# Two transposes of the mixed rows moved ahead of two weight chunks, and one pair of copies moved ahead of another

## The chip, the cores and the metric

The kernel runs on one core of one Trainium2 chip. The metric is the device time of one execution, in microseconds. The core has five engines that run their own instruction lists and meet through semaphores: TensorE (PE in the profile, its weight loads PEld), VectorE (DVE), ScalarE (ACT), GpSimd (POOL) and SyncE (SP), which here only issues DMAs.

## The reference, cut to what matters

```python
x = L0_attn_x                                  # (2, 1024, 128): two sequences
xn = _layernorm(x)
s = _L0_attn_ref(xn, ...)                      # gated recurrence with a scan over time
g = _silu(_L0_ffn_ref(xn, ...))                # six layers of local attention and FFN
return x + s * g

# inside _L0_ffn_ref, for each of the 6 layers
x = attn_layer(shift_tokens(x), Wqkv[i], q_scale[i], k_scale[i], Wo[i]) + x
x = ffn_layer(shift_tokens(x), ln_g[i], ln_b[i], W1[i], b1[i], W2[i], b2[i]) + x

def shift_tokens(t):        # the second half of the columns comes from the token before
    a, s = jnp.split(t, 2, -1)
    s = jnp.pad(s, ((0, 0), (1, 0), (0, 0)))[:, :-1]
    return jnp.concatenate([a, s], -1)
# attn_layer: qkv = x @ Wqkv (128 -> 3 * 1024), 16 heads of 64, l2norm and rotary on q and k,
# softmax within windows of 32 tokens and the window before, times v, @ Wo
```

Everything is computed in float32; the products for q, k, v and the first FFN product are made of three products of split operands (high and low parts).

## The kernel before, in words

The two sequences are two streams, b = 0 and 1. Each is cut into 8 tiles of 128 tokens. A step i is one tile of one layer, so there are 48 steps, and each step has two halves, one for each stream. Every engine has a function half(i, b) that writes out its work of that half by hand, in order; the engine executes it in that order. The stages of the pipeline lie side by side: in half (i, b) TensorE makes q, k, v of tile i (qkv, six chunks of 512 columns: 0 and 1 are q, 2 and 3 are k, 4 and 5 are v), transposes k and q of tile i - 1 (transpose_keys, transpose_qk) and makes its scores, transposes the probabilities of tile i - 2 (transpose_probs), multiplies them with v (probs_v) and projects (out_projection), and does the FFN of tile i - 4 (ffn_up, down_chunks). From step 40 on the recurrence of the other branch is worked in (the rec_ functions).

The "mixed rows" are the tile of x with the shifted half of its columns. SP copies the shifted half in with three DMAs (shift_x, x<-x in the profile) in the half before. transpose_mixed(i, b) transposes them for the next half: stream 1 of the same step in the half of stream 0, stream 0 of the next step in the half of stream 1 (next_tile). ScalarE's evac_mixed copies the transpose out twice, as xsh and rounded as xs_hi; GpSimd's low_x makes the low part xs_lo, and with that chunk 0 of the next half may start.

PSUM banks are handed out in pairs by written orders. tr_order is that of the two banks ps_tr: in each half probs 0, probs 1, qk 2, qk 3, mixed, qk 0, qk 1, and "rows" in stream 1. The n-th fill takes bank n % 2, and TensorE waits in ring_free until the fill before it in the same bank has been copied out (tr_done). pv_order does the same for ps_pv and qn_order for ps_qn (chunks 0 to 5, with the recurrent ones between 3 and 4). Neither order is changed.

Of the other functions named below: evac_k copies the transposed keys out of ps_tr (kT, L1184), evac_pv the result of P times V (oT, L1175), evac_q the transposed queries (qT, L1195), square writes the squares of a chunk (sq, L1166), exps is ScalarE's exponential of the scores (L1201). VectorE's rotate reads a chunk twice (t and qk, L1535 and L1538) once square has been done, and so frees its bank. ffn_gate (hid, L1661) is its product in the FFN, which frees the bank of ffn_up. On GpSimd the two additions of a half (qk, L2016), the scalings (qkr, L2028) and floor (floored, L1986) matter here.

Of the kernel before, what the change touches and what calls it, by code (L numbers as in the profile page):

```python
# [91 lines left out]
def valid(step):  # L92

    return not step.fixed or 0 <= step.n < STEPS
# [269 lines left out]
def layers(nc, a, x, xmid, branch, ident, eps_col, w, rec):  # L364

    with ExitStack() as ctx:
# [145 lines left out]
        def first_half(i, b):  # L512
            return i.first and b == 0
# [37 lines left out]
        with nc.Block() as block:  # L551
# [191 lines left out]
            def _(pe):  # L743
# [30 lines left out]
                def qkv(i, b, chunks):  # L774
                    if not valid(i):
                        return
                    if 0 in chunks:
                        pe.wait_ge(xs_ready[b], i.n + 1)
                    if not first_half(i, b):
                        pe.wait_ge(lo_ready[chunks[0] // 2], (i.layer + 1) * w.splits(chunks[0] // 2))  # L780
                    for c in chunks:
                        if first_half(i, b) and c == 1:
                            transpose_input([1], ps_pv[1])
                        if first_half(i, b):

                            part = c // 2
                            pe.wait_ge(*((lo_ready[part], w.splits(part)) if c % 2 else (lo_ready[part], 1) if part == 2 else (first_low, part + 1)))
                        bank = next_bank(i, ("qkv", b, c))
                        place = w.split_place(i.layer, c // 2, c % 2)
                        part = slice(place, place + COLS)  # L790
                        mm(ps_qn[bank][:, :], xs_hi[b][:, :], w_hi[:, part], start=True, stop=False)  # L791
                        mm(ps_qn[bank][:, :], xs_hi[b][:, :], w_lo[:, part], start=False, stop=False)  # L792
                        mm(ps_qn[bank][:, :], xs_lo[b][:, :], w_hi[:, part], start=False, stop=True).then_inc(qn_full[bank], 1)  # L793
# [67 lines left out]
                def probs_v(i, b, f):  # L861
                    j = i - 2
                    if not valid(j):
                        return
                    if j.first:
                        pe.wait_ge(s_xT, 6)
                        pe.wait_ge(cleared, 1)
                    if f == 0:
                        pe.wait_ge(v_moved[b], (j.n + 1) * V_MOVE)
                        pe.wait_ge(v_carried[b], (j.n + 1) * V_CARRY)  # L870
                    wait_fill(pe, tr_done, tr_order, i, ("probs", b, f))
                    bank, n = fill(pv_order, i, ("pv", b, f))
                    ring_free(pe, pv_done, bank, n)
                    for g in (2 * f, 2 * f + 1):
                        for w in range(WINDOWS):
                            for hp in (2 * g, 2 * g + 1):
                                last = mm(pv_target(bank, hp, w), v_win[b][:, w, hp * DH:(hp + 1) * DH],  # L877
                                          pbd[:, hp, :, WINDOW * w:WINDOW * (w + 1)], start=True, stop=True)
                    last.then_inc(pv_full[bank], 1)
# [127 lines left out]
                def half(i, b):  # L1007
                    transpose_probs(i, b, 0)
                    transpose_probs(i, b, 1)
                    qkv(i, b, (0, 1))  # L1010
                    if (i.n, b) == (1, 1):
                        transpose_pair(1)
                    out_projection(i, 1 - b)
                    transpose_keys(i, b)
                    if b == 0:
                        probs_v(i, b, 0)
                        probs_v(i, b, 1)
                    qkv(i, b, (2, 3))
                    if b == 1:
                        probs_v(i, b, 0)  # L1020
                        probs_v(i, b, 1)
                    if i.first and b == 0:
                        pe.wait_ge(s_xT, 1)
                        transpose_input(range(B, HEAD), ps_pv[0])
                    transpose_mixed(i, b)
                    mask(i, b)
                    rec_hidden(i, b)
                    rec_gate_projection(i, b)
                    if (i.n, b) == (1, 1):
                        transpose_pair(2)  # L1030
                    transpose_qk(i, b, 0)
                    rec_output(i, b)
                    rec_rates(i, b)
                    transpose_qk(i, b, 1)
                    if b == 0:
                        ffn_up(i, 0)
                        ffn_up(i, 1)
                    qkv(i, b, (4, 5))
                    if (i.n, b) == (1, 0):
                        transpose_pair(0)  # L1040
                    if b == 0:
                        ffn_up(i, 2)
                    else:
                        transpose_rows(i)
                    scores(i, b, 0)
                    scores(i, b, 1)
# [63 lines left out]
            def _(act):  # L1110
# [257 lines left out]
                def half(i, b):  # L1368
                    new_layer = i.t == TILES - 1 and b == 1 and not i.last_layer
                    root_first = b == 0 and (i.t > 0 or i.first)  # L1370
                    if root_first:
                        inverse_root(*norm_tile(i, b), i - 3)
                    evac_probs(i, b, 0)
                    if not root_first and not i.first:
                        inverse_root(*norm_tile(i, b), i - 3)
                    square(i, b, 0)
                    evac_probs(i, b, 1)
                    square(i, b, 1)
                    if not root_first and i.first:
                        inverse_root(*norm_tile(i, b), i - 3)  # L1380
                    if i.first and b == 0:
                        split_first(4)
                        split_first(5)
                    if (i.n, b) in ((1, 0), (1, 1)):
                        normalise_pair(2 * b)
                    exps(*softmax_tile(i, b))
                    if new_layer:
                        split_high(i.layer + 1, 0)
                    evac_k(i, b, 0)
                    evac_k(i, b, 1)  # L1390
                    if b == 1:
                        square(i, b, 2)
                        square(i, b, 3)
                        normalise_rows(i)
                    evac_pv(i, b, 0)
                    evac_pv(i, b, 1)
                    if b == 0:
                        square(i, b, 2)
                    evac_mixed(i, b)
                    if b == 0:  # L1400
                        square(i, b, 3)
                    if b == 0 and valid(i - 4):
                        nc.scalar.preload_act_table(ACT.Gelu)
                    rec_gelu(i, b)
                    rec_decay(i, b)
                    rec_output(i, b)
                    evac_q(i, b, 0)
                    rec_tanh(i, b)
                    if b == 0:
                        ffn_gelu(i, 0)  # L1410
                    evac_q(i, b, 1)
                    if b == 0:
                        ffn_gelu(i, 1)
                    evac_v(i, b, 4)
                    if b == 0:
                        ffn_gelu(i, 2)
                    if (i.n, b) == (0, 1):
                        input_guess(1)
                    if (i.n, b) == (3, 0):
                        softplus_exp()  # L1420
                    evac_v(i, b, 5)
                    if b == 0 and valid(i - 4):
                        nc.scalar.preload_act_table_set("natural_log_exp_and_others")
                    if b == 1:
                        evac_rows(i)
                    rec_beta_log(i, b)
                    rec_beta_half(i, b)
                    if new_layer:
                        split_high(i.layer + 1, 1)
                    if b == 1:  # L1430
                        if i.t == 3:
                            round_w1(i.layer)
                        if i.t in (5, 6) and not i.last_layer:
                            split_high(i.layer + 1, 2, i.t - 5)
                    if (i.n, b) == (1, 0):
                        normalise_pair(1)
# [840 lines left out]
```

## Time and profile before

| | |
|---|---|
| median of 3 runs | 1550.27 us (1549.19 to 1552.37) |
| the profiled execution | 1548.62 us |
| its span, first to last instruction | 1546.8 us |
| TensorE busy | 1499.9 us, 97% |
| ScalarE, GpSimd, VectorE busy | 1346.7, 1291.4, 1283.4 us |
| mean granted clock of TensorE | 0.995 |

The profile lists instructions with the line of the kernel, the engine, and output<-inputs. "Busy" is the time in which an instruction of the engine runs; the ends of matmuls are modelled and overlap the starts of the next, so the starts say more than the ends. A row of the timeline has start, duration, engine, line, and behind it in brackets the idle time of the engine before it and the instruction that ended it.

### The profile page before, as it was taken

The numbers are of one execution on the slowest core, as the hardware profiler recorded it, in microseconds if no ns is written. First come the engines' busy times: TensorE is split into PE (matmuls) and PEld (weight loads), VectorE is DVE, ScalarE is ACT, GpSimd is POOL, SyncE is SP. The second block draws the span as 40 slices with busy tenths as digits, with TensorE's granted clock in tenths as the row PEclk, the third lists the DMA queues.
The fourth block names the chain that finished last, engine by engine and source line by source line (L and its number), as shares of the span: only waits on it lengthen the run. The fifth ranks groups of instructions, "written<-read, shape, count | busy, mean of one in ns | idle before, by whom it ended". The sixth has DMA issues, their size and how long they took to land.

```text
span 1546.8 us, 64269 instructions
## 1 busy us (share of the span) xinstructions
PE 1499.9 (97%) x26170; PEld 1306.7 (84%) x26170; DVE 1283.4 (83%) x2033; ACT 1346.7 (87%) x2600; POOL 1291.4 (83%) x1268
## 2 busy tenths in 40 slices
PE   6899999999999999999999999999999999999996
PEld 3688888888888888888888888888888888888885
DVE  7888888888889878788878878887888878888876
ACT  5779998999998889898989999889899889989974
POOL 8899899978889888899888899888989977767741
PEclk8999999999999999999999999999999999999999
DMA  5344433454343444434354433444433333333232
GB/s 142 88 111 118 100 83 89 103 128 109 87 103 73 101 118 123 96 86 102 74 128 117 102 90 88 101 101 124 108 89 89 86 76 96 91 80 74 65 91 57
DMA packets 219395, 150.44 MB, mean 97 GB/s; under 512 B 144604, under 2 KB 166752, under 8 KB 219104
## 3 DMA queue, kind: packets, MB, share of 16 engines
q1 hardware_dynamic: 219104, 146.33, 39.2%
q8 instruction: 211, 3.46, 1.0%
q14 instruction: 80, 0.66, 0.1%
HBM read 27.50 MB, written 1.05 MB: 18 GB/s over the span
## 4 chain that ended last, share of the span: by engine, by line
PE 81%; issue 5%; POOL 5%; DVE 4%; ACT 4%; SPq 1%; DMA 0%; POOLq 0%; ACTq 0%; DVEq 0%
PE ps_pv L877 11%; PE ps_tr L816 10%; PE ps_pv L909 9%; PE ps_qn L791 8%; PE ps_s L856 8%; PE ps_qn L793 7%; PE ps_qn L792 7%; PE ps_tr L803 5%; PE ps_pv L889 3%; PE ps_s L838 2%; PE ps_pv L927 2%; POOL qk L2016 2%; PE ps_pv L929 2%; PE ps_pv L928 2%; POOL qkr L2028 1%
## 5 line engine op out<-in xcount | busy, mean ns | idle before, releaser
L2016 POOL TENSOR_TENSOR qk<-qk,t 128x1024 f32<-128x1024 f32 x192 | 459.8, 2395 | 1.6 <-ACT v_new L1249 1.1
L2028 POOL TENSOR_TENSOR qkr<-qk,rinv 128x1024 f32<-128x1024 f32 x192 | 363.9, 1907 | 3.7 <-POOL rinv L2000 0.2
L1535 DVE TENSOR_TENSOR t<-ps_qn,tab 128x512 f32<-128x512 f32 x384 | 260.8, 679 | 87.3 <-ACT sq L1166 79.0
L791 PE MATMUL ps_qn<-w_hi,xs_hi 128*128 128x512 f32 x576 | 252.8, 439 | 16.0 <-DVE qk L1538 12.1
L1538 DVE TENSOR_TENSOR qk<-ps_qn,tab 128x512 f32<-128x512 f32 x384 | 261.2, 680 | 0.0
L1166 ACT ACTIVATE sq<-ps_qn 128x512 f32<-128x512 f32 x384 | 229.6, 599 | 27.7 <-PE ps_qn L793 17.9
L1154 ACT ACTIVATE pbd<-ps_tr 64x512 f32<-64x512 f32 x384 | 225.7, 588 | 12.2 <-PE ps_tr L803 8.8
L793 PE MATMUL ps_qn<-w_hi,xs_lo 128*128 128x512 f32 x576 | 229.1, 398 | 0.0
L792 PE MATMUL ps_qn<-w_lo,xs_hi 128*128 128x512 f32 x576 | 228.9, 397 | 0.0
L1548 DVE TENSOR_REDUCE ss<-sq 128x32 f32<-128x2048 f32 x96 | 218.4, 2275 | 0.0
L816 PE MATMUL ps_tr<-ident,qkr 128*128 128x128 f32 x1536 | 210.6, 274 | 5.8 <-ACT pbd L1154 2.5
L877 PEld LDWEIGHTS ps_pv<-pbd,v_win 128*64 128x64 f32 x6144 | 187.5, 138 | 25.2 <-issue 24.7
L816 PEld LDWEIGHTS ps_tr<-ident,qkr 128*128 128x128 f32 x1536 | 175.2, 141 | 34.0 <-issue 18.2
L877 PE MATMUL ps_pv<-pbd,v_win 128*64 128x64 f32 x6144 | 200.9, 224 | 0.0
L2038 POOL TENSOR_TENSOR pr<-pr,rrec 128x1024 f32<-128x1024 f32 x96 | 183.4, 1911 | 16.3 <-issue 11.1
L909 PE MATMUL ps_pv<-wo,oT 128*128 128x128 f32 x1536 | 187.2, 275 | 1.4 <-DVE oT L1555 1.4
L909 PEld LDWEIGHTS ps_pv<-wo,oT 128*128 128x128 f32 x1536 | 182.6, 192 | 6.0 <-DVE oT L1555 1.2
L1561 DVE TENSOR_REDUCE rmax<-ps_s 128x16 f32<-128x1024 f32 x96 | 117.1, 1220 | 67.0 <-PE ps_s L856 64.4
L856 PE MATMUL ps_s<-kT,qT 64*32 64x64 f32 x12288 | 151.7, 225 | 5.2 <-issue 4.8
L856 PEld LDWEIGHTS ps_s<-kT,qT 64*32 64x32 f32 x12288 | 135.1, 105 | 23.5 <-issue 22.3
L791 PEld LDWEIGHTS ps_qn<-w_hi,xs_hi 128*128 128x128 f32 x576 | 109.4, 190 | 46.7 <-issue 16.8
L1986 POOL TENSOR_SCALAR floored<-ss 128x34 f32<-128x34 f32 (+1 forms) x96 | 30.1, 313 | 121.3 <-DVE ss L1617 108.2
(178 smaller groups left out, 3024.8 us busy)
## 6 DMA issues: line engine op xcount, KB each, us to landing
v_win<-v_new SPq DMA_DIRECT2D x576, 128.0 KB
v_win<-v_new SPq DMA_DIRECT2D x192, 64.0 KB
v_win<-v_win SPq DMA_DIRECT2D x188, 64.0 KB, 2.0
kT<-kT SPq DMA_DIRECT2D x84, 128.0 KB, 2.7
w_raw<-in_Wqkv SPq DMA_DIRECT2D x18, 512.0 KB, 3.9
rot<-in_rot SPq DMA_DIRECT2D x48, 128.0 KB, 3.5
wo<-in_Wo SPq DMA_DIRECT2D x6, 512.0 KB, 4.7
x<-x SPq DMA_DIRECT2D x48, 56.0 KB
```

Source lines behind the costliest of these rows:

```text
L791: mm(ps_qn[bank][:, :], xs_hi[b][:, :], w_hi[:, part], start=True, stop=False)
L792: mm(ps_qn[bank][:, :], xs_hi[b][:, :], w_lo[:, part], start=False, stop=False)
L793: mm(ps_qn[bank][:, :], xs_lo[b][:, :], w_hi[:, part], start=False, stop=True).then_inc(qn_full[bank], 1)
L816: last = tr(ps_tr[bank][:, m * P:(m + 1) * P], qkr[b][:, (4 * f + m) * P:(4 * f + m + 1) * P], ident[:, :])
L856: last = mm(ps_s[q, h, hp, :], qT[rows, hp, q], kT[b][rows, hp, WINDOW * w:WINDOW * (w + 2)], start=False, stop=hp == HP - 1)
L877: last = mm(pv_target(bank, hp, w), v_win[b][:, w, hp * DH:(hp + 1) * DH], pbd[:, hp, :, WINDOW * w:WINDOW * (w + 1)], start=True, stop=True)
L909: last = mm(ps_pv[bank][:, 0:P], oT[:, n // 2, n % 2, :], wo[:, n, :], start=(n == 0), stop=(n == HP - 1))
L1166: f(sq[:, c * COLS:(c + 1) * COLS], ps_qn[bank][:, :], ACT.Square).then_inc(squared[b], 1)
L1535: v.tensor_tensor(t2[:, part].rearrange("p (h s d) -> p h s d", s=2, d=DH // 2), swapped, tab[:, 2 * k + 1:2 * k + 2, :].rearrange("p o (s ...
L1538: v.tensor_tensor(qk[b][:, part].rearrange("p (h d) -> p h d", d=DH), ps_qn[bank][:, :].rearrange("p (h d) -> p h d", d=DH), tab[:, 2 * k: ...
L2016: g.tensor_tensor(qk[b][:, part], qk[b][:, part], t2[:, part], ALU.add).then_inc(added[b], 1)
L2028: g.tensor_tensor(qkr[b][:, part].rearrange("p (h d) -> p h d", d=DH), qk[b][:, part].rearrange("p (h d) -> p h d", d=DH), rinv[b][:, k * ...
```

## The change

On TensorE, transpose_mixed(i, b) goes in front of chunks 2 and 3 in both halves, except in the very first half. In stream 0 it stands behind P times V (probs_v) then, in stream 1 directly behind transpose_keys. On ScalarE, evac_mixed goes in front of evac_pv 0 and 1 in stream 0, except in step 0; in stream 1 ScalarE's order is as before.

```diff
@@ TensorE, half(i, b)
                     if b == 0:
                         probs_v(i, b, 0)
                         probs_v(i, b, 1)
+                    if not (i.first and b == 0):
+                        transpose_mixed(i, b)
                     qkv(i, b, (2, 3))
                     if b == 1:
                         probs_v(i, b, 0)
@@
                     if i.first and b == 0:
                         pe.wait_ge(s_xT, 1)
                         transpose_input(range(B, HEAD), ps_pv[0])
-                    transpose_mixed(i, b)
+                    if i.first and b == 0:
+                        transpose_mixed(i, b)
                     mask(i, b)
@@ ScalarE, half(i, b)
                         normalise_rows(i)
+                    if b == 0 and not i.first:
+                        evac_mixed(i, b)
                     evac_pv(i, b, 0)
                     evac_pv(i, b, 1)
                     if b == 0:
                         square(i, b, 2)
-                    evac_mixed(i, b)
+                    if b == 1 or i.first:
+                        evac_mixed(i, b)
                     if b == 0:
                         square(i, b, 3)
```

## Rows read from the trace of the kernel before

**Rows 1.** Busy time by stretch: PE, PEld, DVE, ACT, POOL, clock, DMA share, GB/s.
```profile
20.00:40.00 20.00, 14.15 (x53) 9.07 (x51) 18.18 (x44) 10.88 (x29) 17.61 (x20) 0.83 0.30 76
...
240.00:1200.00 960.00, 954.57 (x17167) 839.19 (x17162) 804.47 (x1220) 864.88 (x1644) 845.50 (x811) 1.00 0.42 101
```
**Rows 2.** Timeline of TensorE, an ordinary stream 1 half (step 26).
```profile
797.49 1.04 PE L816 MATMUL ps_tr<-ident,qkr 128*128 128x128 f32 x8
798.28 0.48 PE L791 MATMUL ps_qn<-w_hi,xs_hi 128*128 128x512 f32 x1
...
801.86 0.33 PE L757 MATMUL ps_tr<-ident,x 128*128 128x128 f32 x1
802.03 0.59 PE L838 MATMUL ps_s<-mask_bf,sel_bf 128*128 128x512 bf16 x2
802.46 1.29 PE L816 MATMUL ps_tr<-ident,qkr 128*128 128x128 f32 x8
```
**Rows 3.** Timeline of ScalarE, the same half.
```profile
798.18 1.09 ACT L1184 ACTIVATE kT<-ps_tr 128x512 f32<-128x512 f32 x2
...
802.04 0.60 ACT L1175 ACTIVATE oT<-ps_pv 128x512 f32<-128x512 f32 x1 [0.24 <-PE ps_pv L877]
...
802.69 0.28 ACT L1127 ACTIVATE xs_hi<-ps_tr 128x128 fp32r<-128x128 f32 x1
```
**Rows 4.** Timeline of TensorE's weight loads, the same half.
```profile
803.09 0.42 PEld L816 LDWEIGHTS ps_tr<-ident,qkr 128*128 128x128 f32 x4 [0.27 <-issue]
```
**Rows 5.** The copy of the key transposes, one line's instructions: min/median/max ns.
```profile
L1184 ACT ACTIVATE kT<-ps_tr x192: 577/593/603, 36.8 to 1496.3; 128x512 f32<-128x512 f32 x192
```
**Rows 6.** Timeline of ScalarE, stream 1 halves of steps 4 and 46.
```profile
134.39 1.09 ACT L1184 ACTIVATE kT<-ps_tr 128x512 f32<-128x512 f32 x2 [0.18 <-PE ps_tr L816]
...
1432.69 1.09 ACT L1184 ACTIVATE kT<-ps_tr 128x512 f32<-128x512 f32 x2 [0.36 <-PE ps_tr L816]
```
**Rows 7.** Timeline of ScalarE and TensorE, stream 1 half behind a new layer.
```profile
738.40 1.08 ACT L1184 ACTIVATE kT<-ps_tr 128x512 f32<-128x512 f32 x2
...
739.08 0.50 PE L791 MATMUL ps_qn<-w_hi,xs_hi 128*128 128x512 f32 x1 [0.18 <-DVE qk L1538]
```
**Rows 8.** Timeline of SP's DMA issues, ahead of the half of rows 2.
```profile
795.39 0.69 SPq L298 DMA_DIRECT2D x<-x  x1
```
**Rows 9.** The page's DMA issues: count, KB each, us to landing.
```profile
kT<-kT SPq DMA_DIRECT2D x84, 128.0 KB, 2.7
```
**Rows 10.** Timeline of TensorE, the stream 0 half that follows.
```profile
813.88 0.50 PE L791 MATMUL ps_qn<-w_hi,xs_hi 128*128 128x512 f32 x1
...
815.39 0.27 PE L757 MATMUL ps_tr<-ident,x 128*128 128x128 f32 x1
815.50 0.59 PE L838 MATMUL ps_s<-mask_bf,sel_bf 128*128 128x512 bf16 x2
...
818.92 0.40 PE L791 MATMUL ps_qn<-w_hi,xs_hi 128*128 128x512 f32 x1
```
**Rows 11.** Timeline of ScalarE, the same stream 0 half.
```profile
812.22 1.08 ACT L1184 ACTIVATE kT<-ps_tr 128x512 f32<-128x512 f32 x2
...
814.89 0.60 ACT L1166 ACTIVATE sq<-ps_qn 128x512 f32<-128x512 f32 x1 [0.24 <-PE ps_qn L793]
...
816.03 0.60 ACT L1166 ACTIVATE sq<-ps_qn 128x512 f32<-128x512 f32 x1
```
**Rows 12.** Timeline of VectorE, the same stream 0 half.
```profile
817.40 0.68 DVE L1538 TENSOR_TENSOR qk<-ps_qn,tab 128x512 f32<-128x512 f32 x1
818.94 0.48 DVE L1661 SCALAR_TENSOR_TENSOR hid<-ps_pv,b,hid 128x256 f32<-128x256 f32 x1 [0.86 <-ACT hid L1241]
```
**Rows 13.** The waits: engine, line, releaser, us in total, times, longest.
```profile
POOL floored L1986 <- DVE ss L1617: 108.2, 45, 5.4
```
**Rows 14.** Timeline of VectorE and TensorE, stream 0 half of a recurrent step.
```profile
1423.23 0.98 DVE L1661 SCALAR_TENSOR_TENSOR hid<-ps_pv,b,hid 128x256 f32<-128x256 f32 x2
...
1424.17 0.28 PE L927 MATMUL ps_pv<-fxn_hi,w_hi 128*85 128x256 f32 x1
```

## The prediction

> **What bounds the kernel now.** I read the busy time by stretch first, then the timeline of each engine over one ordinary step, then the waits. Between 240 and 1200 us TensorE works 954.57 of 960 us at a granted clock of 1.00, and the next busiest, ScalarE, 864.88 [rows 1]. So in the steady part anything that makes TensorE wait is added to the time, one for one, and a wait that goes away can give back at most those 5.4 us there, unless it is hidden inside a busy record. One such hidden wait exists: in stream 1 the eight query transposes take 1.29 us (802.46), where a run of eight without a wait takes 1.04 (the key transposes at 797.49) [rows 2]. The weight load of the second four starts only at 803.09, 0.12 us after the copy of the mixed rows (802.69 and 0.28) ends [rows 3, 4]. It is 0.25 us in each stream 1 half, some 11 us in all, and it is the only thing in the neighbourhood that a better order could win.
>
> One step is two halves, stream 0 and stream 1, about 30 us together. In each, TensorE works through its list in order. The lists differ: in stream 0 P times V stands between the key transposes and chunk 2, in stream 1 chunk 2 follows the key transposes directly.
>
> **Stream 1: the transpose in front of chunk 2.** The mixed transpose writes a bank of ps_tr. The order of fills in a half is probs 0, probs 1, qk 2, qk 3, mixed, qk 0, qk 1 over two banks, so mixed takes the bank of the first four key transposes (qk 2), and transpose_mixed first waits until ScalarE has copied those (evac_k 0). Before, that wait had three products of chunk 2, three of chunk 3 and all of P times V in front of it and never ended last. Now it stands immediately behind the key transposes.
>
> When does that copy end? The key transposes start at 797.49 and chunk 2 starts at 798.28, so TensorE is free for the next thing 0.79 us after their start [rows 2]. The copy starts at 798.18 [rows 3]: it needs the fourth transpose finished and cannot be earlier. One copy takes 0.59 us (median of 192) [rows 5], so it ends at 798.78, 0.50 us after TensorE would be free. This is the fixed geometry of these two instructions: in the first and the last of the 43 stream 1 halves from step 4 to step 46, ScalarE idles 0.18 and 0.36 us before this copy, waiting for the transposes [rows 6], so nothing on ScalarE can make it earlier. From the end of a copy of this kind to the weight load behind it the trace shows 0.12 us [rows 3, 4], and the transpose starts about 0.02 later: 0.14. The transpose itself then keeps TensorE for 0.17 us when its weight load is exposed (801.86 to 802.03) and 0.11 when it is not (815.39 to the mask's start) [rows 2, 10]; I take 0.14. Chunk 2 therefore starts 0.50 + 0.14 + 0.14 = 0.78 us later. Everything queued behind the waiting transpose goes with it: chunks 2 and 3, and P times V.
>
> Does stream 1 get the 0.17 us back where the transpose stood? No. The second four query transposes still wait for evac_mixed, and in stream 1 the copies keep their order on ScalarE: evac_pv 0, evac_pv 1, evac_mixed. evac_pv 1 starts at 802.04, when P times V has ended [rows 3]. So the restart of TensorE stays a fixed 1.2 us behind the end of P times V, and the 0.17 us only lengthens the stall of 0.25. The half as a whole is later by the full 0.78.
>
> 43 halves × 0.78 = 33.5 us. Ten of them, at the ends and starts of layers, have ScalarE late as well. In the worst, the copy starts at 738.40 and ends at 739.0, where TensorE was free at about 738.0; there chunk 3 already waits for VectorE until 739.08, so part is covered [rows 7]: about 0.96 instead of 0.78. For all ten I add 1.8. The stream 1 halves of steps 0 to 3 run while TensorE waits for other things anyway (14.15 of 20 us busy between 20 and 40 us [rows 1]); between nothing and 4 us, I take 2.
>
> The transpose also needs the shifted rows, and SP issues their last DMA in the half before. In the step shown it is issued at 795.39 [rows 8]; the transpose is now wanted from 798.28 and can't run before 798.9 in any case. The nearest transfer with a landing time, a copy inside SBUF of the keys, takes 2.7 us [rows 9], which is 798.1. I cost it at nothing; what covers it is the wait for evac_k, 0.8 us of it. At 0.5 us for a landing that is later in every third half it would be 7 us.
>
> **Stream 0: both orders.** Here P times V (2 us) stands between the key transposes and the mixed one, so evac_k 0 (812.22 and 0.6) is long done at 813.88 [rows 10, 11] and the bank is free. On TensorE only the neighbours change: the mixed transpose pays 0.17 behind P times V instead of 0.11 behind chunk 3, and chunk 2's first product 0.48 behind a transpose [rows 2] instead of 0.50 [rows 10]. That is +0.04 in 46 halves, 1.8 us, with bounds of 0 and 0.1.
>
> ScalarE now waits with evac_mixed until that transpose ends, about 814.25, where before it started evac_pv 0 at about 813.2. From there evac_mixed takes 0.33, the two copies of P times V 0.48 each, square 2 then starts at about 815.54 instead of 814.89, and square 3 behind it at about 816.1. It was 816.05 before, since before ScalarE waited three times for TensorE on this way and now once [rows 11]. So ScalarE is 0.1 us late behind it, VectorE's rotation of chunks 2 and 3 0.65. That rotation ended at 818.08 and now ends at 818.73; chunk 5 is wanted at 818.92 in the same bank [rows 10, 12]. It just fits. Behind it VectorE had 0.86 us idle before the gate of the FFN (818.94) [rows 12], which absorbs the 0.65. GpSimd's second addition is up to 0.5 late and is absorbed too: it idles 108.2 us in 45 waits, 2.4 each, before the next floor [rows 13]. In six recurrent steps VectorE has no idle there: the first gate (1423.23, about 0.45 long) would end at 1424.33, and with 0.14 release ffn_up 2 at 1424.47 instead of 1424.17 [rows 14]. 6 × 0.3 = 1.8 us.
>
> **Given back.** A later TensorE shortens waits on engines that were late independently of it. The whole of such idle time between 240 and 1200 us is 5.4 us [rows 1]; I take 2.
>
> **Sum.** 33.5 + 1.8 + 2 + 1.8 + 1.8 − 2 = 38.9 us. The profiled execution took 1548.62 us (span 1546.8), giving 1587.5. The median of the runs shown is 1.65 us above it: 1550.27 + 38.9 = 1589.
>
> On the clock there is a rule that speaks against this change: the Trainium skill, page "TensorE: Matmul & The Clock Gate", section "A second HAM failure mode: psum-queue depth-cycling", says that a TensorE which pauses often and shortly while it cycles through PSUM banks can swing between its two clock levels. The new wait is a pause of just that kind. Here the granted clock fell to a mean of 0.83 over a stretch in which TensorE was busy 14.15 of 20 us; in the steady part it is 1.00, and the new pauses would leave TensorE busy about 97% there [rows 1]. My sum leaves the clock at 2.4 GHz; by the rule it would be larger by what the clock rival below gives.
>
> **The rivals.**
> Faster: the earlier transpose lets evac_mixed run earlier and the 0.25 us stall of each stream 1 half goes. 44 × 0.25 gives 1539. For it: the stall is real [rows 2, 4]. Against it: in stream 1 ScalarE's order is untouched, so the copy can't start before evac_pv 1, and the new wait costs 0.64 before it could win 0.25. It decides only if TensorE does not stop for evac_k, that is, if the copy ended 0.5 us earlier. Chance 3%.
> No change: the wait is hidden or the traffic of stream 0 gives it back: 1550. It would need slack on TensorE that the busy times don't have. 3%.
> Worse than the forecast: VectorE's late rotation in stream 0 also holds chunk 5. The margin is 0.19 minus a release of 0.05 to 0.14. If each stream 0 half loses 0.2 to 0.4 us more, 39 × 0.3 = 12 us, 1601. 10%.
> Smaller: the start and stream 0 cost nothing (5.6 us less) and 5 us are given back instead of 2: 1580; with 0.1 us less in each restart, 1576. 12%.
> The clock: were it 0.83 as between 20 and 40 us through the steady part, 955 × (1/0.83 − 1) adds about 196 us, 1785. 1%.
>
> **The numbers.** The forecast, with 71%, is 1589 with its own range of 1582 to 1596. The range that takes in the bounds of the restart (0.70 to 0.85 per half), of stream 0 (0 to 0.2) and of the start is 1574 to 1602. A measurement of this kernel can tell about 0.2%, 3 us, from no change. Faster 3%, the same 4%, slower 93%.
>
> **What would show it.** In the profile after: in stream 1 a gap between the key transposes and the mixed one, ended by ScalarE's kT copy, of about 0.64 us; TensorE's waits list it with some 45 times and close to 30 us; TensorE's busy share near 95%; the eight query transposes of stream 1 still with their stall, up to 0.4 us; in stream 0 no such gap, ScalarE idle about 1 us before xsh, VectorE's rotation 0.65 late, no wait before chunk 5; steps of about 30.6 instead of 29.8 us. I am wrong if that gap is missing or shorter, if chunk 5 waits, or if the shifted rows end the gap in place of the copy.

## The result, and the profile after

The changed kernel takes 1581.03 us (median of 4 runs, 1579.52 to 1584.05), the kernel before 1549.73 us beside it (median of 4, 1548.05 to 1552.37). The ratio is 1.0202, with a 95% interval of 1.0188 to 1.0217: 31.3 us slower. The forecast was 1589 and 38.9 us, with its own range of 1582 to 1596 and the whole range 1574 to 1602. Sign and mechanism were right, and the size was 8 us too big: the time lies 1 us below the forecast's own range and inside the whole one. The profiled execution of the changed kernel took 1584.05 us (span 1582.3), 3.0 us over its median; the one of before lies 1.1 us under this median of before. So differences between the two traces come out about 4 us larger than those between the medians.

Lines of the page of after: busy time by engine, and the engines' shares of the chain that ended last.
```profile
PE 1508.3 (95%) x26170; PEld 1299.0 (82%) x26170; DVE 1282.8 (81%) x2033; ACT 1337.2 (85%) x2600; POOL 1290.0 (82%) x1268
...
PE 78%; ACT 8%; issue 7%; POOL 4%; DVE 2%; DMA 0%; SPq 0%; ACTq 0%; POOLq 0%; DVEq 0%
```
Busy time by stretch of after, the same columns as [rows 1].
```profile
20.00:40.00 20.00, 13.15 (x42) 8.77 (x43) 17.09 (x42) 9.89 (x27) 17.60 (x20) 0.77 0.31 78
240.00:1200.00 960.00, 937.95 (x16738) 813.38 (x16739) 786.04 (x1193) 840.19 (x1611) 827.92 (x801) 1.00 0.41 100
```
The amount of work is the same. Between 240 and 1200 us TensorE is now busy 937.95 of 960 us, where it was 954.57 [rows 1], with the clock still at 1.00. The change has put waits into TensorE's list, and the waits view says which.

The waits of after: engine, line, releaser, us in total, times, longest. First those of TensorE's matmuls, then one of ScalarE's and one of the weight loads.
```profile
PE ps_tr L757 <- ACT kT L1187: 23.8, 47, 2.3
...
PE ps_tr L816 <- ACT xs_hi L1130: 8.3, 38, 0.5
...
PE ps_qn L975 <- DVE qk L1544: 2.8, 7, 1.2
```
```profile
ACT xsh L1129 <- PE ps_tr L757: 53.1, 47, 1.4
PEld ps_tr L757 <- ACT kT L1187: 35.1, 47, 2.6
```
The top row of waits is new: the mixed transpose (L757) waits for the copy of the first key transposes (kT) once in each stream 1 half. The matmul's idle time is 23.8 us, 0.51 each. The weight load's is 35.1, 0.75 each, since the modelled end of the transposes before covers part of the matmul's.

TensorE in a stream 1 half of after (step 26); beside it ScalarE.
```profile
815.02 1.04 PE L816 MATMUL ps_tr<-ident,qkr 128*128 128x128 f32 x8
816.37 0.33 PE L757 MATMUL ps_tr<-ident,x 128*128 128x128 f32 x1 [0.31 <-ACT kT L1187]
816.47 0.47 PE L791 MATMUL ps_qn<-w_hi,xs_hi 128*128 128x512 f32 x1
...
820.50 0.60 PE L816 MATMUL ps_tr<-ident,qkr 128*128 128x128 f32 x4
821.31 0.63 PE L816 MATMUL ps_tr<-ident,qkr 128*128 128x128 f32 x4 [0.21 <-ACT xs_hi L1130]
821.70 0.48 PE L791 MATMUL ps_qn<-w_hi,xs_hi 128*128 128x512 f32 x1
```
```profile
815.72 1.09 ACT L1187 ACTIVATE kT<-ps_tr 128x512 f32<-128x512 f32 x2
817.45 1.30 ACT L1169 ACTIVATE sq<-ps_qn 128x512 f32<-128x512 f32 x2 [0.64 <-PE ps_qn L793]
...
820.23 0.60 ACT L1178 ACTIVATE oT<-ps_pv 128x512 f32<-128x512 f32 x1 [0.24 <-PE ps_pv L877]
820.73 0.27 ACT L1129 ACTIVATE xsh<-ps_tr 128x128 f32<-128x128 f32 x1
820.88 0.28 ACT L1130 ACTIVATE xs_hi<-ps_tr 128x128 fp32r<-128x128 f32 x1
```
Chunk 2 starts 816.47 − 815.02 = 1.45 us after the key transposes, where it was 0.79 [rows 2]: 0.66 us. The query transposes show the old stall made longer: they start at 820.50 and the next chunk at 821.70, 1.20 later (1.04 before), with the second four still released by xs_hi. So the 0.17 us that the mixed transpose no longer takes behind P times V is lost in the stall. The median length of a step, taken over 34 steps between 175 and 1200 us, went from 29.97 to 30.60 us; 30.6 was forecast.

TensorE, ScalarE and VectorE in the stream 0 half of the same step of after, which runs ahead of the stream 1 half.
```profile
799.32 2.08 PE L877 MATMUL ps_pv<-pbd,v_win 128*64 128x64 f32 x64
801.34 0.33 PE L757 MATMUL ps_tr<-ident,x 128*128 128x128 f32 x1
801.42 0.48 PE L791 MATMUL ps_qn<-w_hi,xs_hi 128*128 128x512 f32 x1
...
806.33 0.42 PE L791 MATMUL ps_qn<-w_hi,xs_hi 128*128 128x512 f32 x1
```
```profile
801.70 0.28 ACT L1129 ACTIVATE xsh<-ps_tr 128x128 f32<-128x128 f32 x1 [1.26 <-PE ps_tr L757]
...
802.99 1.12 ACT L1169 ACTIVATE sq<-ps_qn 128x512 f32<-128x512 f32 x2
```
```profile
803.72 0.69 DVE L1541 TENSOR_TENSOR t<-ps_qn,tab 128x512 f32<-128x512 f32 x1 [2.27 <-ACT sq L1169]
```
Here TensorE has no gap, ScalarE idles 1.26 us before xsh, and the rotation starts 4.40 us after P times V. In before it was 3.72: 0.68 later, where 0.65 was forecast. The two rows of before:
```profile
811.87 2.08 PE L877 MATMUL ps_pv<-pbd,v_win 128*64 128x64 f32 x64
...
815.59 0.69 DVE L1535 TENSOR_TENSOR t<-ps_qn,tab 128x512 f32<-128x512 f32 x1 [1.48 <-ACT sq L1166]
```

### The profile page after: what moved, and what is told of

It reads as the page before. It is cut to its first block, busy times and chain, and to the rows that moved or that the text cites. A ratio compares the mean times of both kernels' runs of the same rounds, so it can differ in the third digit from the quotient of the medians.

```text
span 1582.3 us, 64269 instructions
## 1 busy us (share of the span) xinstructions
PE 1508.3 (95%) x26170; PEld 1299.0 (82%) x26170; DVE 1282.8 (81%) x2033; ACT 1337.2 (85%) x2600; POOL 1290.0 (82%) x1268
## 3 DMA queue, kind: packets, MB, share of 16 engines
q8 instruction: 211, 3.46, 1.0%
HBM read 27.50 MB, written 1.05 MB: 18 GB/s over the span
## 4 chain that ended last, share of the span: by engine, by line
PE 78%; ACT 8%; issue 7%; POOL 4%; DVE 2%; DMA 0%; SPq 0%; ACTq 0%; POOLq 0%; DVEq 0%
PE ps_pv L877 11%; PE ps_pv L909 9%; PE ps_tr L816 8%; PE ps_s L856 8%; PE ps_qn L791 8%; PE ps_qn L793 7%; PE ps_qn L792 7%; PE ps_tr L803 5%; PE ps_pv L889 3%; PE ps_pv L927 2%; PE ps_pv L928 2%; PE ps_pv L929 2%; ACT kT L1187 2%; PE ps_tr L757 2%; POOL qkr L2034 1%
## 5 line engine op out<-in xcount | busy, mean ns | idle before, releaser
L1169 ACT ACTIVATE sq<-ps_qn 128x512 f32<-128x512 f32 x384 | 226.0, 607 | 48.0 <-PE ps_qn L793 37.5
L791 PE MATMUL ps_qn<-w_hi,xs_hi 128*128 128x512 f32 x576 | 251.5, 437 | 12.7 <-DVE qk L1544 9.6
L816 PEld LDWEIGHTS ps_tr<-ident,qkr 128*128 128x128 f32 x1536 | 177.0, 142 | 39.1 <-issue 23.8
L791 PEld LDWEIGHTS ps_qn<-w_hi,xs_hi 128*128 128x128 f32 x576 | 112.2, 195 | 37.5 <-issue 12.5
```

The source lines that it names most:

```text
L816: last = tr(ps_tr[bank][:, m * P:(m + 1) * P], qkr[b][:, (4 * f + m) * P:(4 * f + m + 1) * P], ident[:, :])
L1169: f(sq[:, c * COLS:(c + 1) * COLS], ps_qn[bank][:, :], ACT.Square).then_inc(squared[b], 1)
```

## The experiments

All ratios are to the kernel before on the same chip. "Per half" numbers behind a run are taken over the 33 to 35 halves of each stream between about 175 and 1200 us, of the time from the start of one group of TensorE's instructions to the start of the next; they are my sums over the timeline. For the scores they are means. For the stretches ahead of the scores in stream 1 they are medians, since a few halves at the edges of layers differ: the mean from the keys to chunk 2 is 0.82 in before and 1.55 in after, the median 0.79 and 1.45.

**1. Stream 1 alone.** Only TensorE's move in stream 1.
```diff
+                    if b == 1:
+                        transpose_mixed(i, b)
                     qkv(i, b, (2, 3))
...
-                    transpose_mixed(i, b)
+                    if b == 0:
+                        transpose_mixed(i, b)
```


> Only stream 1's transpose goes in front of chunks 2 and 3; stream 0 is as before. Theory (TensorE waits there for ScalarE's copy of the first keys, 0.56 us in each stream 1 half, plus 0.10 for the transpose): the whole loss is here, some 47 x 0.66 less what is given back at the layers' ends, +28 to +33 us. Rival (half or more of the loss comes from stream 0, where VectorE's rotation is 0.65 us late): +10 to +18 us.

Measured: 1574.85 us, ratio 1.0153 (1.0136 to 1.0170), +23.7 us. Keys to chunk 2 take 1.45 us in place of 0.79, the query transposes 1.20 in place of 1.05. Stream 1 carries three quarters of the change. That is 4 us less than the lower end of what was expected, and above the rival. In the traces the 43 stream 1 halves behind 128 us lose 27.5 us, nearly as expected, and the 35 ordinary stream 0 halves give back 3.2, which was not.

**2. Stream 0 alone, and 3. its part on TensorE alone.** The same edits under `b == 0`; in the third run ScalarE's order stays as before.
```diff
+                    if b == 0 and not i.first:
+                        transpose_mixed(i, b)
                     qkv(i, b, (2, 3))
...
-                    transpose_mixed(i, b)
+                    if b == 1 or i.first:
+                        transpose_mixed(i, b)
@@ ScalarE, in the second run only
+                    if b == 0 and not i.first:
+                        evac_mixed(i, b)
                     evac_pv(i, b, 0)
```


> Only stream 0's transpose and its copies are moved; stream 1 is as before. Theory (the bank is long free, the late rotation falls into idle time, and only the recurrent steps lose some 0.5 us each): -2 to +3 us. Rival (the late rotation costs in each half): +10 to +20 us.

> Only TensorE's transpose of stream 0 is moved, ScalarE keeps evac_pv, square 2, evac_mixed. Theory: ScalarE no longer waits for the transpose, so its work and VectorE's rotation are as early as before or earlier; the neighbours on TensorE give back 0.04 us in each stream 0 half: -3 to 0 us. Rival (the new place of the transpose itself costs in stream 0): +3 us and more.

Measured: 1557.51 us, 1.0040 (1.0026 to 1.0054), +6.2 us with both; 1551.99 us, 1.0010 (0.9999 to 1.0020), with TensorE's part alone. The first lies 3 us above what was expected and below the rival; the second cannot be told from no change, where up to 3 us faster was expected. Up to chunk 5 a stream 0 half is 0.03 to 0.04 us shorter in both. In the run with ScalarE's part, chunk 5's first product then takes 0.26 us in place of 0.23, and in the recurrent steps TensorE's wait below makes each of seven stream 0 halves longer, six by 0.42 us and the first by 0.71, 0.46 on average. The waits of the run with both name the place:
```profile
PE ps_qn L975 <- DVE qk L1544: 2.8, 7, 1.2
```
In the run without ScalarE's part this row reads 0.6 us, once, in before 0.5 us, once. L975 is the recurrence's rates product (rec_rates); it stands between the two runs of query transposes and takes the bank of chunk 2, which VectorE's rotation frees. In the trace of after, TensorE and VectorE there:
```profile
1450.69 0.66 PE L816 MATMUL ps_tr<-ident,qkr 128*128 128x128 f32 x4
1451.61 0.67 PE L975 MATMUL ps_qn<-w_raw,rec_w_rates 128*128 128x256 f32 x2 [0.26 <-DVE qk L1544]
```
```profile
1450.78 0.68 DVE L1544 TENSOR_TENSOR qk<-ps_qn,tab 128x512 f32<-128x512 f32 x1
```
The rotation of chunk 2 ends at 1451.46 and the product starts at 1451.61, 0.92 us behind the transposes. In the same place of before it was 0.49:
```profile
1417.77 0.66 PE L816 MATMUL ps_tr<-ident,qkr 128*128 128x128 f32 x4
1418.26 0.60 PE L975 MATMUL ps_qn<-w_raw,rec_w_rates 128*128 128x256 f32 x2
```
The seven waits come to 3.2 us, half of the 6.2. What the rest is stays open: the traced execution of this run took 1552.38 us, the fastest of its eight and 5 us under their median.

**4. Behind chunk 2, and 5. the same without the added wait.** The mixed transpose stands between chunks 2 and 3 in stream 1, where the copy of the keys should be done. The split call repeats one wait on the weights, which the fifth kernel leaves out again.
```diff
@@ against after
...
+                        qkv(i, b, (2,))
                         transpose_mixed(i, b)
-                    qkv(i, b, (2, 3))
+                        qkv(i, b, (3,))
@@ the fifth kernel, in qkv
-                    if not first_half(i, b):
+                    if not first_half(i, b) and chunks != (3,):
```


> The changed kernel, but stream 1's transpose stands between chunk 2 and chunk 3. Chunk 2 takes 0.77 us on TensorE, the wait for the copy was 0.56. Theory (the wait for the bank is the cost, not the place ahead of P times V): the 0.56 goes and the 0.10 stays, +0 to +7 us against the kernel before. Rival (TensorE loses by the change of operand types or by restarting, wherever the transpose stands between chunks): +15 us and more.

> The kernel with the transpose between chunks 2 and 3 in stream 1, without the second wait that its split call had added to TensorE's list in each step (48 instructions, which moved the 16 KB blocks in which TensorE's instructions are fetched against its work). Theory (of its 15 us, 0.11 us in each stream 1 half is the move and the rest are stalls of 1 to 2 us within the scores, each at a block's end): +3 to +9 us. Rival (the place between the chunks itself costs it): +13 to +17 us again.

Measured: 1566.29 us, 1.0097 (1.0082 to 1.0113); and 1560.12 us, 1.0065 (1.0054 to 1.0077). The long wait is gone in both: of the 0.66 us per half ahead of the scores 0.11 to 0.12 is left: the transpose's own time between the chunks, while the time it no longer takes behind P times V is lost again in the stall of the query transposes (1.20). The first came out at +15.0 us, 8 over the upper end of what was expected and at the edge of its rival, and 5 us of that went when the 48 waits, all fulfilled long before, were taken out of TensorE's list. The second is at +10.1, 1 us over what was expected and 3 below its rival. What the waits cost is not lost where they stand. It is lost inside the scores, 1.70 us per stream 1 half in place of 1.49 (1.50 without the waits), and unevenly, in a few halves:
```profile
965.21 1.43 PE L856 MATMUL ps_s<-kT,qT 64*32 64x64 f32 x121
968.43 0.31 PE L856 MATMUL ps_s<-kT,qT 64*32 64x64 f32 x7 [1.80 <-issue]
```
Here TensorE waits 1.80 us for no semaphore, seven matmuls ahead of the end of a run of 128. Run 9 takes this up: stops at one place of the list, described in the last section, add up to 14.8 us in the first of these kernels and to 7.8 in the second, as in before. What the second of these kernels still loses in its trace is 2.9 us in the stream 1 halves of the steady part, about 4 in the recurrent steps, and 5.7 up to 128 us, more than any other kernel here in that stretch.

**6. The copy in front of the transposed keys' made longer, in after and 7. in before.** ScalarE makes one more copy (240 columns, 0.27 us from its start to that of the next) ahead of evac_k 0 in stream 1. If the new wait is the limit, after grows by it, and before does not. The line that makes the buffer and its semaphore is left out below.
```diff
                     act.wait_ge(tr_full[bank], n)
+                    if b == 1 and k == 0:
+                        act.wait_ge(spared, j.n)
+                        f(spare[:, :], ps_tr[bank][:, 0:COLS - 272], ACT.Copy).then_inc(spared, 1)
                     f(kT[b][:, 4 * k:4 * k + 4, WINDOW:],
```


> The changed kernel with one more copy of 240 columns on ScalarE ahead of the copy of the first keys in stream 1. Theory (TensorE waits for exactly that copy): each stream 1 half is later by the whole of the extra copy, 0.25 to 0.35 us, 12 to 16 us more than the changed kernel, some +43 to +48 us against the kernel before. Rival (the shifted rows or the restart set the wait): no more than 3 us above the changed kernel.

> The kernel before with the same extra copy. Theory: there nothing waits for the copy of the first keys before P times V has ended, and ScalarE has 0.24 us idle on the way: 0 to +4 us. Rival (ScalarE is as near to the bound as TensorE, so the extra copy costs anywhere): +12 us and more.

Measured: 1592.09 us, 1.0273 (1.0257 to 1.0288), 11 us over after, 1 us short of the 12 to 16 that were expected; and 1551.65 us, 1.0007 (0.9997 to 1.0017). The wait of the sixth kernel, where the lines are one further:
```profile
PE ps_tr L758 <- ACT kT L1191: 37.3, 47, 3.6
```
It grew by 13.5 us in 47 waits, 0.29 each; from the keys to chunk 2 a half now takes 1.70 us in place of 1.45. The same copy in before costs nothing that can be measured. So it is ScalarE's copy that sets when TensorE restarts, in after alone.

**8. In front of P times V.** The stall of the query transposes is the thing that could be won. TensorE makes the mixed transpose in stream 1 ahead of P times V (six products behind the keys), and ScalarE copies it ahead of evac_pv 0. Stream 0 is as before.
```diff
                     if b == 1:
+                        transpose_mixed(i, b)
                         probs_v(i, b, 0)
...
+                    if b == 1:
+                        evac_mixed(i, b)
                     evac_pv(i, b, 0)
```


> Against the kernel before: in stream 1 the transpose goes behind chunks 2 and 3 and in front of P times V, and ScalarE's evac_mixed in front of evac_pv 0; stream 0 is as before. Theory (the cost of the change is the wait for the bank, and the 0.25 us stall of the second four query transposes is the wait for the copy behind evac_pv 1): the copies of the keys are long done there, and the stall goes, 44 x 0.25, so -8 to -12 us. Rival (the stall only moves, since evac_pv is later now and ends last): -2 to +3 us.

Measured: 1547.08 us, 0.9985 (0.9973 to 0.9997), 2.3 us faster, a quarter of what was expected and just outside the rival's range. The stall is gone:
```profile
800.23 1.04 PE L816 MATMUL ps_tr<-ident,qkr 128*128 128x128 f32 x8
```
The query transposes take 0.82 us to the next start in place of 1.05, and a stream 1 half is 0.29 us shorter ahead of its scores. But the scores take 1.60 us in place of 1.49, and two single stalls of 1.3 and 1.5 us stand in the recurrent steps that before does not have. So the traces show where the gain is given back. They name no semaphore for which the scores wait in the even part of it, and why they stretch is not settled.

**9. Before, with 36 more waits.** To tell apart "the waits cost time where they stand" from "they shift the rest of the list": the first wait of TensorE's program is repeated 36 times. Each is on a semaphore that has its value already. In the trace they are 18 instructions, each with two of these waits (TensorE has 54,025 records in place of 54,007), so the rest of the list is shifted by 18 places, and not by the 36 that the expectation counts with. The 48 waits of run 4 are 48 records.
```diff
-                pe.wait_ge(s_const, 16)
+                for _ in range(37):
+                    pe.wait_ge(s_const, 16)
                 spin_up()
```


> The kernel before with 36 more waits for the identity, long fulfilled, at the head of TensorE's list: every later instruction is 36 places further in the 256-instruction blocks in which the list is fetched. A stall was seen only where a block began more than 200 places into the 256 instructions of a half's scores; with the shift 10 halves have it at 240 or more, in place of 4. Theory (the place of the blocks against the scores sets these stalls): +3 to +8 us, all in single halves, 1 to 2.5 us each. Rival (they come from other traffic and not from the place): within 2 us of the kernel before.

Measured: 1561.23 us, 1.0064 (1.0052 to 1.0076), +10 us, 2 over the upper end of what was expected and far from the rival, from instructions that all stand ahead of TensorE's first matmul (it starts at 6.2 us, in before at 4.2). The expected number of halves with a stall was worked out for a shift of 36 and does not hold; that the position sets the stalls does. Its waits of TensorE on nothing that the profile shows:
```profile
PE ps_tr L803 <- issue: 6.8, 10, 1.7
...
PE ps_s L856 <- issue: 5.8, 6, 1.3
```
In before the same two rows read 0.6 and 4.8 us:
```profile
PE ps_s L856 <- issue: 4.8, 3, 2.3
...
PE ps_tr L803 <- issue: 0.6, 2, 0.4
```
That is 7.2 us of the 10; 1.4 more are there by 100 us. What the stalls are stands in the last section.

**10. Both good halves together, from step 4 on.** Stream 1 as in run 8, stream 0 TensorE's part as in run 3; steps 0 to 3 as before, because the traces of runs 2, 3 and 8 were 0.8 to 2.9 us behind there.
```diff
+                    late = i.n >= 4
+                    if b == 0 and late:
+                        transpose_mixed(i, b)
                     qkv(i, b, (2, 3))
                     if b == 1:
+                        if late:
+                            transpose_mixed(i, b)
...
+                    if b == 1 and late:
+                        evac_mixed(i, b)
                     evac_pv(i, b, 0)
```


> From step 4 on: in stream 1 the transpose in front of P times V with its copies in front of evac_pv 0 (the order that gave 0.16 us in each stream 1 half), in stream 0 TensorE's transpose in front of chunks 2 and 3 with ScalarE's order as before (0.08 us in each stream 0 half). Steps 0 to 3 as before. Theory (both gains are of the steady part, and the changes at the start only cost): 36 x 0.24, -7 to -11 us. Rival (the gains don't add up, because TensorE's own instruction stream sets the pace there): -1 to -4 us.

Measured: 1545.90 us, 0.9964 (0.9952 to 0.9977), 5.6 us faster than before. That is less than the 7 to 11 that were expected and more than the rival's 4. It is the one version that beats both kernels by more than 3 us.

**11. After, from step 4 on.** The whole change, but not in steps 0 to 3, by the same `late`.

> The changed kernel, but with steps 0 to 3 in the order before. Theory (in the first four steps the change costs some 4 us of its own): +25 to +29 us against the kernel before. Rival (what is lost there is given back later, or the other way round): +31 us as the changed kernel.

Measured: 1578.32 us, 1.0177 (1.0164 to 1.0191), +27.4 us, within what was expected. The start is worth 2.4 us in the traces (up to 128 us this kernel is 1.9 us behind before, after 4.3), 0.25% or 3.9 us by the ratios. This term is uncertain by about 2 us: run 10, whose list is that of before in steps 0 to 3, is 2.3 us behind before's trace there as well. The wait, without those steps:
```profile
PE ps_tr L757 <- ACT kT L1188: 17.5, 43, 1.1
```

## Why the prediction was right, and where its size was off

The mechanism held in stream 1, where the cost is, in each of its steps. The gap stands where it was put, is ended by the kT copy 47 times and never by the shifted rows. TensorE is busy 95%, the query transposes kept and lengthened their stall, and stream 0 has no wait behind P times V. The extra copy (runs 6 and 7) shows that this copy is the limit and that it had slack before. Two of the prediction's own signs of being wrong came out, both by a little: the gap is shorter than forecast, 0.56 us from where TensorE was free (815.81) in place of 0.64, and chunk 5 waits, by 0.03 us. The rule on the clock that was weighed did not come into play: the granted clock is 1.00 between 240 and 1200 us, with a pause in each step.

The terms, against what the traces and runs show:

| term | forecast | measured |
|---|---|---|
| stream 1, 43 halves | 0.78 each, 33.5 | 0.66 each, 28.4 |
| late halves and what is given back | +1.8 − 2 | −1.2 |
| steps 0 to 3 | +2 | +2.4 (run 11) |
| ordinary stream 0 halves | +1.8 | −0.8 |
| recurrent stream 0 halves | 6 × 0.3 = 1.8 | 7 × 0.46 = 3.2 |
| sum | 38.9 | 32.0 |

**The step that was mis-sized is the restart of TensorE.** I took 0.50 us for the copy, 0.14 from its end to the transpose and 0.14 for the transpose. The copy is right: it starts at 815.72, 0.70 after the keys, and with 0.59 ends at 816.31. The transpose then starts at 816.37, 0.06 later and not 0.14, and chunk 2 follows at 816.47, 0.10 later and not 0.14. I had read the release from [rows 3, 4] as the time from the copy's end to a weight load, and added 0.02 for the matmul. Here weight load and matmul carry the same start, and the release is less than half as long: in all 47 halves between 0.053 and 0.055 us from the end of the copy. And I had put the transpose between two costs seen with other neighbours; behind a stall it costs less than either. 0.12 us × 43 = 5.2 of the 8 us.

**The ten late halves** cost nothing extra. Taken over 36 stream 1 halves, the loss is 22.6 us, 1.2 less than 36 × 0.66: where ScalarE or VectorE was late at the edge of a layer, the new wait took the place of an old one. TensorE's waits for VectorE before a chunk (L791) fell from 12.1 us in 21 to 9.6 in 11.

**Stream 0** came out near in sum (2.4 us by the trace of after, 3.6 forecast), but by luck, since its two terms were off in opposite ways. I had the transpose dearer behind P times V; it is cheaper (0.10 for 0.11), and chunk 2's first product too (0.31 for 0.34). In after chunk 5 does wait, but by 0.03 us: the margin of 0.19 minus the release was used up. The rival that put 0.2 to 0.4 us there did not come.

**The recurrent steps** have a step with the wrong place. I followed the late rotation to VectorE's gate and from there to ffn_up 2. It is wanted earlier, by rec_rates in the bank of chunk 2, a fill that the order names "between 3 and 4" and that I had passed over. Run 2 shows it with 0.46 us per half, and run 3, without the move on ScalarE, is free of it.

The sum of the right-hand column is 0.7 us over the measured 31.3, but this closeness says little: its start is a difference to run 11, its other rows come from the traces, and these differ by 35.4. There the start takes 4.3 us, the 43 stream 1 halves 27.9, the seven stream 0 halves of steps 40 to 46 2.3, what comes behind step 46 1.4, and the 35 ordinary stream 0 halves give back 0.5. Stalls of the kind of run 9 don't enter: those over 0.35 us add up to 8.0 us in after and 7.8 in before. The rival "smaller" (1576 to 1580, 12%) lay nearer than the forecast: 1 us away, where the forecast is 8 away. Its part on the restart came true (0.12 us less in each), its parts on a free start and a free stream 0 did not. The lower edge of the whole range is wider than the bounds named for it: a restart of 0.70, nothing at the start and no change of neighbours in stream 0 give 1589 − 3.4 − 2 − 1.8 = 1582, which the measured time misses by 1 us.

What stays open: why a stream 1 half that reaches its scores 0.29 us earlier takes 0.11 us more for them (run 8). The single stalls of the last section explain the uneven part alone.

## What to carry to other kernels

An instruction that takes a PSUM bank belongs at least as far behind the filler of that bank as its copy takes: here 1.3 us from the start of eight transposes, so that the same transpose costs 0.66 us per half directly behind them, 0.11 three products later (run 5), and six products later, with its own copy moved as well, the half gains 0.29 ahead of its scores (run 8). Six products later without the copy was not run. When a stage is made late, search the written orders of every resource that it frees, at all steps, for the next taker; the first one in the list decides, not the one that the usual step shows. And where TensorE is busy 97%, compare runs before believing 0.5%: moving nothing but the position of its list, by 18 instructions, was worth 10 us.

## What the runs showed of the hardware

TensorE's list is fetched in pieces, and TensorE stops when a piece comes late. The page of after, DMA queues (packets, MB, share):
```profile
q8 instruction: 211, 3.46, 1.0%
```
3.46 MB in 211 transfers are 16.4 KB each; TensorE has 54,007 records, 256 for each transfer. From 100 us on I took every start in the scores and in the transposes of probabilities behind them that comes over 0.35 us after the one before it. Most lie at one place of each 256 records, number 193 counted from 0: 5 of 9 in before, 7 of 8 in after, 11 of 15 in run 4, 15 of 19 in run 9. In these four traces the others wait for a result of GpSimd (pr). Over the whole list the stops at this place add up to 7.8 us in before (8 of them, one of which is also a wait for VectorE), 14.8 in run 4 (14) and 16.3 in run 9 (17). Most are found where many short instructions have gone before: the 256 weight loads and matmuls of a half's scores start within 1.5 us. In the trace of run 9, right behind them:
```profile
961.77 1.16 PE L856 MATMUL ps_s<-kT,qT 64*32 64x64 f32 x93
...
964.65 1.06 PE L803 MATMUL ps_tr<-ident,pr 128*128 128x128 f32 x8 [1.73 <-issue]
```
What ends such a stall, the trace shows in time: the last fetch ahead of the stall that ended at 1055.96 in run 9 ran from 1053.06 to 1054.58. All 13 traces of this case agree. They have 2730 such places with a fetch ahead of them, and at none does TensorE pass earlier than 1.15 us after the end of that fetch. The 110 that stop it for over 0.35 us end 1.15 to 1.61 us after the fetch; in before the median of those that do not is 5.0. A fetch starts at most 297 records ahead of the one that has to wait for it, and the stalls end 2.2 to 3.2 us after its start. So a boundary costs nothing where these records take longer than that, and stalls TensorE where they fall into the scores. 18 more instructions shift which half's scores a boundary falls into, and with that the time by 10 us. The Trainium skill, page "Runtime: NRT & Kernel Launch", section "Instruction fetch mechanics", says that the list is refilled in blocks of 16 KiB or 256 instructions, ahead of the execution, and that the cost of crossing a boundary is mostly hidden. The size of the block agrees with this trace, and most crossings cost nothing here as well (203 of 211 in before). But the rest is not small: one crossing took 2.5 us (before, at 1491.05), and where they fall decides over 10 us.
